# Graph network on one core: stores of sums, and one stage's loads, issued by ACT instead of SP

## What is computed

```python
# layer 0                                          # layer 1
h = (layernorm(x) @ W.T).reshape(n, 8, 32)         h = (layernorm(x) @ W).reshape(n, 8, 32)
alpha = a_src.h[src] + a_dst.h[dst] \
      + sum(relu(edge_attr @ edge_W.T + b) * h[dst])   e = a1[src] + a2[dst]
attn = softmax over the edges of one dst (leaky_relu(., 0.2))
out = segment_sum(h[src] * attn, dst) + bias       (the same)
x = x + out;  x = x + ffn(layernorm(x))            (the same)
```

## Time and profile before

| | us |
|---|---|
| median of 3 runs (lowest to highest) | 7785.42 (7784.48 to 7786.51) |
| span of the profiled execution | 7807.0 |
| its stretches: plan, node and prologue of the first edge stage | 0 to 469 |
| first edge stage, body | 469 to 3070 |
| its last steps, ffn, node | 3070 to 4500 |
| second edge stage | 4500 to 7090 |
| last ffn | 7090 to 7807 |
| busy: PE 5257.7, DVE 3278.9, POOL 3613.4, ACT 1371.0 | of 7807.0 |

### The profile page before, as it was taken

The page is one execution under the profiler, slowest core; times in us unless marked ns, Lnnn a source line. Parts: engine busy times, 40 slices in busy tenths (PEclk is TensorE's granted clock), DMA queues, the critical chain, the costliest instruction groups (busy, mean ns, idle before and its releaser), DMA issues. The chain is left out here.

```text
span 7807.0 us, 99204 instructions
## 1 busy us (share of the span) xinstructions
PE 5257.7 (67%) x19729; PEld 3739.4 (48%) x19729; DVE 3278.9 (42%) x5938; ACT 1371.0 (18%) x2977; POOL 3613.4 (46%) x3708
## 2 busy tenths in 40 slices
PE   2387887788788878228999625556565556663498
PEld 1144444444444444227999514444444444442498
DVE  6255555555555555721111313333333333336244
ACT  2122222222222222002222200000000000000122
POOL 2635555555555554042222056666666666650222
PEclk9689999999999999658999857777777777786699
DMA  6434444444444443515666544444444444434255
GB/s 220 136 101 122 122 119 123 124 124 125 122 123 121 122 124 102 186 60 165 183 183 183 153 102 114 113 115 115 114 112 113 113 114 116 113 102 154 101 198 188
DMA packets 718013, 1022.24 MB, mean 131 GB/s; under 512 B 301733, under 2 KB 531561, under 8 KB 692608
## 3 DMA queue, kind: packets, MB, share of 16 engines
q0 software_dynamic: 183456, 485.95, 23.8%
q1 hardware_dynamic: 527676, 519.31, 21.7%
q10 hardware_dynamic: 6564, 14.14, 0.5%
HBM read 868.26 MB, written 153.27 MB: 131 GB/s over the span
## 5 line engine op out<-in xcount | busy, mean ns | idle before, releaser
L773 POOL DMA_INDIRECT e_rows<-sc_table,e_eidx x3224 | 3115.9, 966 | 2253.8 <-issue 952.6
L880 PE MATMUL e_ps_o<-e_rows,e_oh 128*128 128x264 f32 x6448 | 1918.5, 449 | 856.9 <-ACT e_res L969 700.8
L880 PEld LDWEIGHTS e_ps_o<-e_rows,e_oh 128*128 128x128 f32 x6448 | 1379.2, 222 | 1384.3 <-issue 1147.6
L1064 DVE SCALAR_TENSOR_TENSOR e_u<-e_encr,e_adst,e_ps_hd 128x512 f32<-128x512 f32 x806 | 597.1, 745 | 1160.2 <-remote 366.1
L1132 DVE TENSOR_TENSOR e_rows<-e_rows,e_ps_w 128x1024 f32<-128x1024 f32 x806 | 970.7, 1207 | 106.3 <-issue 83.5
L822 PE MATMUL e_ps_X<-e_u,e_hwide 128*104 128x512 f32 x1612 | 871.1, 635 | 16.8 <-DVE e_u L1064 14.8
L1055 DVE TENSOR_SCALAR e_ohT<-e_at,e_nid 96x512 bf16<-96x512 int16 x806 | 292.5, 363 | 1384.6 <-DMA e_aw<-sc_a2p 553.7
L969 ACT COPY e_res<-e_ps_o 32x264 f32<-32x264 f32 x806 | 296.0, 367 | 3291.4 <-PE e_ps_o L884 1242.4
L810 PE MATMUL e_ps_enc<-e_at,e_w_enc 96*128 96x512 bf16 x806 | 317.9, 394 | 570.6 <-ACT e_encr L942 383.4
L1676 PE MATMUL x_ps_h<-x_xT,x_w 128*128 128x256 f32 x2624 | 648.2, 405 | 15.4 <-DMA x_b<-in_L_ffn_b_dram 15.4
L1676 PEld LDWEIGHTS x_ps_h<-x_xT,x_w 128*128 128x128 f32 x2624 | 638.5, 337 | 20.6 <-issue 16.4
(11 more groups left out here) (290 smaller groups left out, 3538.7 us busy)
## 6 DMA issues: line engine op xcount, KB each, us to landing
x_w<-in_L_ffn_W_dram SPq DMA_DIRECT2D x112, 1024.0 KB
e_at<-sc_grp SPq DMA_DIRECT2D x403, 192.0 KB
x_w<-in_L_ffn_w_dram SPq DMA_DIRECT2D x60, 1024.0 KB
e_rows<-sc_table,e_eidx POOLq DMA_INDIRECT x3224
e_at<-sc_grp SPq DMA_DIRECT2D x403, 96.0 KB
sc_agg<-e_res SPq DMA_DIRECT2D x816, 33.0 KB
sc_xb<-r_zero SPq DMA_DIRECT2D x24, 1032.0 KB
x_xin<-sc_xb SPq DMA_DIRECT2D x86, 258.0 KB
```

Source lines behind the costliest of these rows:

```text
L773: pool.indirect_dma_start(rows[:, k, s, j, :], None, dr["table"][:, :], bass.IndirectOffsetOnAxis(eidx[:, k, s, j:j + 1], 0)).then_inc(s_r ...
L880: nc.tensor.matmul(ps_o[:, 0:ROW], oh[:, k, at_j:at_j + P], rows[:, k, s, j, :], start=(j == 0), stop=False)
L1064: nc.vector.scalar_tensor_tensor(u[:, p, h, :], encr[:, h, :], adst[:, h:h + 1], ps_hd[:, h, :], ALU.add, ALU.mult).then_inc(s_u, 1)
```

## The change

The stores of sums go from SP to ACT in both edge stages. ACT's `store_behind` stands right behind the eviction of a step and stores the sums of two steps before (`LAG`): wait for its own store before that to have landed, one word of `tab`, one DMA. The eviction doesn't wait for `s_out` any more. In the second stage ACT also issues the two loads of a step (`load_ahead`, behind the store): it waits for the score of 13 steps back, takes two words of `tab` and issues two DMAs for the step 30 ahead of the one evicted (`LEAD` 4 beyond two blocks); the ring of places grows from 5 to 13 (`PLACES`), one semaphore each. Its prologue issues the first 13 steps' loads at once and 17 more behind `place(0, 0)`. SP keeps tables and flags, and in the first stage the loads, with two words a step. The planning stage writes a table of two columns instead of three, so three small stores are gone.

```diff
         N_LD = 32
         N_ROWS = 16 * SB * CH
         EV0, O0, OUT0 = 10, SB, 16
+        LAG, LEAD = 2, 4
         CF, PH = 2 * COLS, 2 * COLS + 2
         PER = 2 if first else 1
         row_of = lambda tile: tile[0:1, :].rearrange("a (h x) -> a h x", h=HEADS)
 
         def ring(s):
-            return s % 4 if s < 12 else 4
+            return s if not first else s % 4 if s < 12 else 4
 
         def loads_of(b, s):
-            return b * (3 * N_LD) + (s // 4 + 1) * N_LD if s < 12 else b * N_LD + N_LD
+            return b * (3 * N_LD) + (s // 4 + 1) * N_LD if first and s < 12 else b * N_LD + N_LD
 
         def kept(s):
             return s % KEEP if s < 2 * KEEP else KEEP
 
-        def since(s):
-            return SB - KEEP if s < KEEP else KEEP if s < 2 * KEEP else SB
-
         def behind(s):
-            return 5 if s < 4 else 4 if s < 12 else SB
+            return SB if not first else 5 if s < 4 else 4 if s < 12 else SB
+
+        why = "the planning stage writes only groups and starts of windows that lie inside their arrays"
+
+        def group_and_node(eng, t):
+            _, vals = nc.values_load_multi_w_load_instructions(tab[0:1, bass.ds(t * 2, 2)], engines=[eng.engine], min_val=0, max_val=NP,
+                                                               skip_runtime_bounds_check_because=why)
+            return (nc.s_assert_within(vals[0], 0, NG - 1, skip_runtime_bounds_check_because=why),
+                    nc.s_assert_within(vals[1], 0, NP, skip_runtime_bounds_check_because=why))
+
+        def first_node(eng, t):
+            _, vals = nc.values_load_multi_w_load_instructions(tab[0:1, bass.ds(t * 2 + 1, 1)], engines=[eng.engine], min_val=0, max_val=NP,
+                                                               skip_runtime_bounds_check_because=why)
+            return nc.s_assert_within(vals[0], 0, NP, skip_runtime_bounds_check_because=why)
+
+        def load(eng, r, g, n):
+            if first:
+                eng.dma_start(at[:, r, :, :].rearrange("q c e -> q (c e)"),
+                              dr["grp"][bass.ds(g, 1), :, :, :].rearrange("a m c e -> a m (c e)").to_broadcast([K3 // PARTS, PARTS, 2 * G])
+                              ).then_inc(s_ld[r], 16)
+                eng.dma_start(hp[:, r, :], dr["hp"][bass.ds(n, WIN), :, :].rearrange("n p d -> (n p) d")).then_inc(s_ld[r], 16)
+            else:
+                eng.dma_start(at[:, r, 0, :], dr["grp"][bass.ds(g, 1), 0, 1, :].to_broadcast([K3, G])).then_inc(s_ld[r], 16)
+                with nc.allow_non_contiguous_dma(reason="eight logits of a node's three parts"):
+                    eng.dma_start(aw[:, r, COLS - HEADS:COLS], dr["a2p"][bass.ds(n, WIN), :, :].rearrange("n p d -> (n p) d")).then_inc(s_ld[r], 16)
+
+        def store(eng, t, s, passed):
+            if not isinstance(t, int) or t > 0:
+                hold(eng, s_out, t * 16 + OUT0, passed)
+            hold(eng, s_ev, t + (1 + EV0), passed)
+            n = first_node(eng, t)
+            eng.dma_start(dr["agg"][bass.ds(n, WIN), :], res[0:WIN, kept(s), :]).then_inc(s_out, 16)
...
-            def store(t, s, n):
-                hold(sp, s_out, t * 16 - (32 * SB - OUT0), s_ps)
-                hold(sp, s_ev, t - (BEHIND - 1 - EV0), s_ps)
-                sp.dma_start(dr["agg"][bass.ds(n, WIN), :], res[0:WIN, kept((s - BEHIND) % SB), :]).then_inc(s_out, 16)
-
             sp.wait_ge(s_ready, 1)
             for b in range(2):
                 tables(b * SB, b)
                 flags(b * SB, b)
             sp.wait_ge(s_nb, 32)
-            for t in range(2 * SB):
-                s = t % SB
-                if t >= behind(s):
-                    sp.wait_ge(s_hd if first else s_xa, (t - behind(s) + 1) * PER)
-                g, n, _ = entry(t)
-                load(ring(s), g, n)
-                if first and t == 3:
-                    sp.wait_ge(s_wp, 1)
-                    for k in range(3):
-                        for i in range(3):
-                            sp.dma_start(w_enc[12 * k + 4 * i:12 * k + 4 * i + 4, :], w_part[:, k, :]).then_inc(s_we, 16)
-                if t == SB + 6:
-                    sp.wait_ge(s_lk, 1)
-                    sp.wait_ge(s_dn, 2)
-                    tables(2 * SB, 0)
-            sp.sem_inc(s_out, OUT0)
+            if first:
+                for t in range(2 * SB):
+                    s = t % SB
+                    if t >= behind(s):
+                        sp.wait_ge(s_hd, (t - behind(s) + 1) * PER)
+                    g, n = group_and_node(sp, t)
+                    load(sp, ring(s), g, n)
+                    if t == 3:
+                        sp.wait_ge(s_wp, 1)
+                        for k in range(3):
+                            for i in range(3):
+                                sp.dma_start(w_enc[12 * k + 4 * i:12 * k + 4 * i + 4, :], w_part[:, k, :]).then_inc(s_we, 16)
+                    if t == SB + 6:
+                        sp.wait_ge(s_lk, 1)
+                        sp.wait_ge(s_dn, 2)
+                        tables(2 * SB, 0)
+            else:
+                sp.wait_ge(s_lk, 1)
+                sp.wait_ge(s_dn, 2)
+                tables(2 * SB, 0)
             steps = steps_of(sp)
 
             def phase(b, k):
                 for s in range(SB):
-                    t = b * SB + (2 * SB + s)
-                    hold(sp, s_hd if first else s_xa, t * PER - (behind(s) - 1) * PER, s_ps)
-                    g, n, back = entry(t)
-                    load(ring(s), g, n)
-                    store(t, s, back)
+                    t = b * SB + s
+                    if first:
+                        ahead = t + 2 * SB
+                        hold(sp, s_hd, ahead * PER - (behind(s) - 1) * PER, s_ps)
+                        g, n = group_and_node(sp, ahead)
+                        load(sp, ring(s), g, n)
                     if s == 2:
                         hold(sp, s_z, b + 1, s_ps)
-                        flags(t - 2, k)
+                        flags((b + 2) * SB, k)
                     if s == 6:
                         hold(sp, s_lk, b + 2, s_ps)
                         hold(sp, s_dn, b * 2 + 4, s_ps)
-                        tables(t + (SB - 6), 1 - k)
+                        tables((b + 3) * SB, 1 - k)
 
             phase(0, 0)
             with sp.Fori(0, steps) as i:
                 for q in range(2):
                     phase(i * 2 + (1 + q), 1 - q)
-            for j in range(BEHIND):
-                t = steps * (2 * SB) + (3 * SB + j)
-                _, _, back = entry(t)
-                store(t, j % SB, back)
-            hold(sp, s_out, steps * (32 * SB) + (16 * SB + 16 * BEHIND + OUT0), s_ps)
...
             def evict(b, s):
                 t = b * SB + s
                 hold(act, s_o, t + (1 + O0), s_pa)
-                if not isinstance(t, int) or t + BEHIND - 2 * SB + 1 >= since(s):
-                    hold(act, s_out, t * 16 + 16 * (BEHIND - 2 * SB + 2 - since(s)), s_pa)
                 nc.scalar.copy(res[0:WIN, kept(s), :], ps_o[0:WIN, 0:ROW]).then_inc(s_ev, 1)
 
-            def phase(b, k, pre, turn, turns):
+            def store_behind(b, s):
+                t = b * SB + s - LAG
+                if not isinstance(t, int) or t >= 0:
+                    store(act, t, (s - LAG) % SB, s_pa)
+
+            def load_ahead(b, s):
+                t = b * SB + (2 * SB + s + LEAD)
+                hold(act, s_xa, t - (SB - 1), s_pa)
+                g, n = group_and_node(act, t)
+                load(act, ring((s + LEAD) % SB), g, n)
+
+            def phase(b, k, pre, turn, turns, ahead):
                 m, n = b + 1, b + 2
                 for s in range(SB):
                     evict(b, s)
+                    store_behind(b, s)
+                    if not first and ahead:
+                        load_ahead(b, s)
                     if first and pre:
                         relu(n, s)
                     if turn and s == 1:
...
                     if turn and s == 10:
                         place(m, 1 - k)
 
+            act.sem_inc(s_out, OUT0)
             if first:
                 for s in range(SB):
                     relu(0, s)
+            else:
+                act.wait_ge(s_nb, 32)
+                for t in range(SB):
+                    g, n = group_and_node(act, t)
+                    load(act, ring(t), g, n)
             sources(0, 0, 0)
             leak(0)
             fade(0)
...
             if first:
                 for s in range(SB):
                     relu(1, s)
+            else:
+                for t in range(SB, 2 * SB + LEAD):
+                    act.wait_ge(s_xa, t - SB + 1)
+                    g, n = group_and_node(act, t)
+                    load(act, ring(t % SB), g, n)
             steps = steps_of(act)
-            phase(0, 0, True, True, 0)
+            phase(0, 0, True, True, 0, True)
             with act.Fori(0, steps) as i:
-                phase(i * 2 + 1, 1, True, True, i + 1)
```

(38 more changed lines are left out.)

16 lines of the change are left out of this document (2 added, 14 removed).

## The result

The changed kernel takes 7957.82 us (median of 4 runs, 7948.37 to 7975.68), the one before 7784.95 (4 runs). The ratio is 1.0231, 95% interval 1.0212 to 1.0249: slower by about 173 us. The profiled execution has a span of 7952.5 us against 7807.0.

What follows compares the result with a forecast made beforehand. It took the first edge stage as bound by a PE and ACT chain through relu 0, the second as nearer POOL's gather floor. +190 + 0 - 30 + 0 = +160 us on the 7785 median gave 7945 us, range 7660 to 8185.

Steps and rivals of the forecast that it cites:

- Sources of the time: First edge stage: a PE and ACT chain through relu 0; the sums' signal is late beside dense gathers, not the store.
- 1.3 us from eviction to relu 0: Sign in the first edge stage that the forecast is right: this spacing on ACT, instead of 0.27 us.
- The first stage near 2790 us: Sign that the forecast is right: the first edge stage takes about 2790 us.
- a second stage 30 us shorter: Sign that the forecast is right: the second edge stage takes near 2560 us.
- POOL's idle time near 10 us: Sign in the second stage's prologue that the forecast is right: POOL's idle near 10 us, before 40.4.
- First stage, +190: ACT's store block between eviction and relu 0 adds 1.0 us a step, partly hidden: +190 us, bounds 0 and +560.
- Second stage, 0 with bounds -60 and +130: Second edge stage: ACT's store and load blocks mostly hide in its idle time, earlier loads help: 0 us.
- Prologue, -30: Second stage's prologue: ACT issues the first 13 loads at once, cutting POOL's idle: -30 us, ends 0 and -40.
- Plan stage, ends, 0: Three small table stores fall away, and the last eviction sets the epilogue: 0 us, plan stage's ends 0 and -4.
- Rival A: Both edge stages: SP bounds each step, so relieving it makes the kernel faster, 7670 us; chance 0.20.
- Rival B: Edge stages: the block after the eviction hides behind PE's late signal, no change, 7775 us; chance 0.08.
- Rival C: Edge stages: slow issue beside gathers, 0.7 us an operation, hits ACT too, far slower, over 8900 us; chance 0.14.

Runs made afterwards that it cites:

- The three copies: The changed kernel plus three small ACT copies of one row between store and relu 0 in each first-stage step: 8043 us, ratio 1.0340.
- the edit in step 1 alone: The changed kernel with second-stage store and loads behind `sources` and `leak` in step 1 of a block only: 7877 us, ratio 1.0132.

## Why the prediction was right, and where it was not

The forecast was 7945 us and slower; 7958 was measured. The side was right, and so was the mechanism of the first stage. The total was right by luck: all of the loss was forecast in the first stage, and more than half of it came in the second. Against the terms the first stage came out 123 us lower, the second 81 higher and the prologue 25 higher, and these errors nearly cancelled.

- **Sources of the time.** "The first stage is a chain over PE and ACT", with relu 0 on it: right. Moving the store behind the relus gives back 53 us of the run with the same instructions. "The late thing is the signal of the sums ... and not the store": right, since the first stage without any store takes the same 2606 us, and its evictions still start late (318 us in all behind the modelled ends of the sums, 359 before). Of the signs named in advance, 1.3 us from eviction to relu 0 came true (1.34). The first stage near 2790 us (2670), a second stage 30 us shorter (it is 76 longer) and POOL's idle time near 10 us (35.5) did not.
- **First stage, +190: the term that was most off.** The block's length was right (1.0 us predicted, 1.06 measured; 284 and 322 ns for its two large parts, beside 0.28 and 0.34). The share was not: I took 56%, the steps in which PE waits for a relu, less 15%, and the body shows 17% of 396 us, the runs 21%. (The 209 waits were counted in 2510 us, which hold 361 steps and not 374; that changes the share little.) A wait that occurs in 56% of steps does not mean that a delay costs in 56% of them. The quick steps grew and the slow ones shrank: the lowest quarter of step lengths ends at 6.48 us instead of 5.34, the highest begins at 7.57 instead of 8.12. The slack was the lateness of the sums' signal: 182 of its 359 us went when relu 0, and with it PE, came later. Why the signal is less late then is not shown. The three copies took only 30 us more of it and cost over half of their time.
- **Second stage, 0 with bounds -60 and +130.** Measured +81, inside the bounds. I had named the place ("ahead of `sources` and `leak` at step 1", at most 105 us) and then let "later steps catch up" take it away. They don't take in 3.0 us: the edit in step 1 alone brings back 72. Blocks were 3.0 us, within the 1.9 to 3.4 given.
- **Prologue, -30.** Measured -5. I took SP's 9.1 us a step for SP's own. ACT's is the same, see the last section.
- **Plan stage, ends, 0:** -4 at the start and +6 at the end, where ACT's last stores wait one behind the other (three issues of `sc_agg` from 7224.13 take 5.14 us).
- **Rival A (SP is the bound)** fell: the first body takes 2606 us with SP relieved (2604 before), the second 2317 and 2312 with SP out of it and ACT's blocks last (2319). Its sum had a slip: half way from 6.19 to 5.0 us is 0.6 and not 0.67 a step, 240 us; and its 7670 appears as 7660 in the range. Neither matters for the outcome. **Rival B** is where the slack comes from, part of a mechanism, not the result. **Rival C** did not come for the single store; its mechanism exists for loads.

## What to carry to other kernels

A queue that never waits is not the bound until somebody is seen to wait for it on the path; relieve it in a trial and look at its consumers: here its wait went from 40.3 to 570.6 us for no gain. An instruction put on another engine costs by what stands behind it there, so put issuing behind the work that others wait for, and look at the rare, block-level step as well as at the common one: here one step in thirteen held nearly all of a stage's loss. A wait counted in the profile gives neither the whole price of a delay nor its slope: the same place charged about a fifth for the first microsecond and over half for the next 0.4 us.

## What the runs showed of the hardware

Slow issuing beside dense gathers belongs to the moment and not to SP. ACT issues the first 13 steps' loads of the second stage with no wait between them. POOL's gathers run from 4559.0 us on. The loads of the first eight steps start within 14.5 us all the same, the last five 9.1 to 10.5 us apart, as SP's did in the earlier trace rows. After a pause of 35 us for other work two come 1.5 us apart, beside gathers just as dense, and then the slow pace returns. The last gather ends at 4688.8, and from 4704.4 on the steps lie 1.5 to 1.8 us apart:

```profile
4569.22 0.32 ACTq L662 DMA_DIRECT2D e_at<-sc_grp  x1
...
4571.53 0.70 ACTq L662 DMA_DIRECT2D e_at<-sc_grp  x1
...
4581.38 0.69 ACTq L662 DMA_DIRECT2D e_at<-sc_grp  x1
...
4590.46 0.01 ACTq L662 DMA_DIRECT2D e_at<-sc_grp  x1
...
4657.58 0.32 ACTq L662 DMA_DIRECT2D e_at<-sc_grp  x1
...
4659.09 0.32 ACTq L662 DMA_DIRECT2D e_at<-sc_grp  x1
...
4667.94 0.70 ACTq L662 DMA_DIRECT2D e_at<-sc_grp  x1
...
4707.89 0.32 ACTq L662 DMA_DIRECT2D e_at<-sc_grp  x1
...
4709.41 0.32 ACTq L662 DMA_DIRECT2D e_at<-sc_grp  x1
```

So the gathers alone do not make an issue slow; loads that were issued and have not yet been served are the other candidate, which no run tested.

POOL idles 35.5 us ahead of its gather there, instead of 40.4:

```profile
4724.23 0.94 POOL L774 DMA_INDIRECT e_rows<-sc_table,e_eidx  x1 [35.47 <-PE e_ps_o L885]
```

In the bodies ACT is slow in this way mostly with the loads. Instructions of its queue that take 0.65 to 0.75 us come 1.36 times a step in the second stage of the change, 0.57 with the loads alone there, 0.25 with the stores alone, and never in the first stage with one store a step. They are as frequent (1.37) in the kernel with all blocks last, whose second body is back at 2317 us, so in the bodies it is the place where they stand that costs. Why a stream of such loads slows the queue that issues it was not settled.

The Trainium skill ("DMA: Bandwidth & Descriptors", Issuing engines are not separate DMA queues) says that issuing from several engines saves the sequencer's time alone. The trace of the first stage agrees: SP's queue had time to spare (570.6 us of waits), and nothing else got faster.

A load of one word of `tab` into a register took ACT 284 ns in the median of 806, one of two words 601 ns in the median of 407. The Trainium skill ("DMA: Bandwidth & Descriptors", Latency and other measured facts) has about 600 ns as a floor for `tensor_load`. The one-word loads lie at half of it.
